# In two layer norms, the copy that forms the second 16-bit part of each row moves from ScalarE to GpSimd

## What is computed

```python
edge_index = jnp.stack([src, dst])
xn = _layernorm(x, axis=-1)
x = x + _L0_gnn_ref(xn, edge_index, ...) + _L0_mix_ref(xn[None], ...)[0]
x = x + _L0_ffn_ref(_layernorm(x, axis=-1)[None], ...)[0]
xn = _layernorm(x, axis=-1)
x = x + _L1_gnn_ref(xn, edge_index, ...) + _L1_mix_ref(xn[None], ...)[0]
x = x + _L1_ffn_ref(_layernorm(x, axis=-1)[None], ...)[0]
return x
```

## Time and profile before

| | us |
|---|---|
| median of 3 runs | 4698.83 (4697.29 to 4701.39) |
| the profiled execution | 4690.14 |
| its span in the trace | 4688.2 |
| PE busy | 3698.4 (79% of the span) |
| DVE busy | 2192.3 (47%) |
| ACT busy | 1351.2 (29%) |
| POOL busy | 744.5 (16%) |

### The profile page before, as it was taken

How to read it: one execution, slowest core, us unless ns; L and a number is a source line. 1 busy time by engine, 2 the same in 40 slices (tenths; PEclk the granted TensorE clock), 3 DMA queues, 4 the chain that set the end, 5 groups by cost and what they waited for, 6 DMA issues and landing times. The chain is left out here.

```text
span 4688.2 us, 90793 instructions
## 1 busy us (share of the span) xinstructions
PE 3698.4 (79%) x23358; PEld 2637.5 (56%) x23359; DVE 2192.3 (47%) x5705; ACT 1351.2 (29%) x2984; POOL 744.5 (16%) x1224
## 2 busy tenths in 40 slices
PE   4888864899699989972464539749989899789998
PEld 2444433566388579651344326529879544457776
DVE  7888878888700221251253420260040577723333
ACT  2555632777600100320010212330000125233333
POOL 3222200000000000017323460200000365200000
PEclk9999975778799899975787769869999999989999
DMA  2111220322244035111010121214425200010000
GB/s 104 49 74 74 93 83 0 97 86 86 86 154 150 32 125 190 35 26 43 11 53 4 41 26 42 92 69 173 165 93 186 73 1 1 5 29 7 13 13 27
DMA packets 128991, 318.06 MB, mean 68 GB/s; under 512 B 46782, under 2 KB 80045, under 8 KB 114376
## 3 DMA queue, kind: packets, MB, share of 16 engines
q1 hardware_dynamic: 113664, 300.41, 18.4%
q0 software_dynamic: 11808, 9.68, 1.6%
q10 hardware_dynamic: 3404, 6.53, 0.4%
HBM read 244.26 MB, written 72.46 MB: 68 GB/s over the span
## 5 line engine op out<-in xcount | busy, mean ns | idle before, releaser
L555 PE MATMUL ps<-hot_key,hot_src 128*126 128x512 bf16 (+1 forms) x2208 | 416.4, 314 | 38.9 <-DVE hot_key L520 20.9
L520 DVE TENSOR_SCALAR hot_key<-col_iota,run_keys 128x625 bf16<-128x625 int16 x1104 | 393.9, 379 | 0.0
L2437 PE MATMUL ps<-xnT,ew 128*128 (+2 forms) x640 | 208.8, 482 | 203.9 <-issue 120.8
L1336 PE MATMUL ps<-gnn_u_thirds,near 125*128 125x256 bf16 x3000 | 336.0, 275 | 23.1 <-issue 23.1
L1336 PEld LDWEIGHTS ps<-gnn_u_thirds,near 125*128 125x128 bf16 x3000 | 330.4, 141 | 27.0 <-issue 24.7
L555 PEld LDWEIGHTS ps<-hot_key,hot_src 128*126 128x126 bf16 x2208 | 212.4, 136 | 234.3 <-DVE hot_key L520 171.6
L2437 PEld LDWEIGHTS ps<-xnT,ew 128*128 128x128 f32 x640 | 132.6, 213 | 274.9 <-issue 151.7
L2312 POOL DMA_INDIRECT rows_room<-node_table,src_idx x256 | 260.9, 1019 | 141.3 <-issue 141.3
L517 DVE TENSOR_SCALAR hot_src<-col_iota,run_srcs 128x125 bf16<-128x125 int16 x828 | 211.6, 256 | 97.0 <-PE ps L555 56.1
L864 PE MATMUL ps<-row_hot,slot_hot 128*128 128x512 f16 x1088 | 221.4, 356 | 3.1 <-DVE row_hot L1077 2.6
L2471 PE MATMUL ps<-table_thirds,rows_room 125*128 125x144 bf16 x1728 | 127.7, 231 | 108.9 <-issue 67.7
(11 more groups left out here) (564 smaller groups left out, 6655.2 us busy)
## 6 DMA issues: line engine op xcount, KB each, us to landing
near<-adjacency SPq DMA_DIRECT2D x80, 1562.5 KB, 6.6
adjacency<-counts SPq DMA_DIRECT2D x125, 312.5 KB, 2.2
own_in<-own_rows SPq DMA_DIRECT2D x34, 512.0 KB, 4.0
expert_rows<-rows_y SPq DMA_DIRECT2D x75, 125.0 KB
rows_room<-expert_rows SPq DMA_DIRECT2D x25, 375.0 KB
pair_in<-high_rows SPq DMA_DIRECT2D x34, 256.0 KB
pair_in<-low_rows SPq DMA_DIRECT2D x34, 256.0 KB
agg0a_adj<-adjacency SPq DMA_DIRECT2D x5, 1562.5 KB, 9.7
```

Of the source, the lines that this page charges most:

```text
L520: nc.vector.tensor_scalar(hot_key[:, j, :], col_iota[:], run_keys[:, ds(at, 1), j:j + 1].rearrange("p a j -> p (a j)"), None, ALU.is_equal ...
L555: last = nc.tensor.matmul(sums[:, b:e], hot_src[:, j, :], hot_key[:, j, b:e], start=False, stop=True, skip_group_check=True)
L1336: last = nc.tensor.matmul(ps[:, j, 0:width], lead_tiles[BUF[j]][:, k, :], parts.thirds[:, k, i, :], start=(k == 0 and i == 0), stop=(k == ...
L2437: last = nc.tensor.matmul(ps[:, piece % 2, 0:n], w1[i][:, c, m * 128:(m + 1) * 128], xnT[:, c, ds(g * NG + first, n)], start=(c == 0), sto ...
```

## The change

ACT no longer makes the second part. POOL gets an instruction list in these two stages: for each tile it waits until the remainder is made, copies it rounded to bf16, and signals DVE. The operands, the semaphores and DVE's instructions are the same.

```diff
                         if t >= 1:
                             b = t - 1
-                            act.wait_ge(left_out, b + 1)
-                            nc.scalar.activation(third(1, b), parts.left[:, b % TG, :],
-                                                 ACT.Copy).then_inc(second_out, 1)
                             act.wait_ge(transposed, b + (TG + 1))
                             nc.scalar.activation(xnT[:, :, b * P:(b + 1) * P],
...
-                if pool_program:
+                if parts:
+                    @block.gpsimd
+                    def _(pool):
+                        for t in range(T):
+                            pool.wait_ge(left_out, t + 1)
+                            nc.gpsimd.tensor_copy(third(1, t), parts.left[:, t % TG, :]).then_inc(second_out, 1)
+                elif pool_program:
                     block.gpsimd(pool_program)
```

## The result

The changed kernel takes 4683.12 us, median of 6 runs (4678.27 to 4686.86), against 4698.32 for the kernel before in the same comparison (4694.38 to 4702.94, 6 runs): a ratio of 0.9968, with a 95% interval of 0.9958 to 0.9978, or 15.2 us less. It was forecast at 4684.0, with a range of 4680.5 to 4692.

A forecast was written before the change was run, and what follows sets the result against it. ACT was taken to bound both norms; without its copy ACT and DVE each need 1.06 us per tile, saving 7.6 us per norm, 15.2 in all. From median 4698.83 to 4683.6, with jitter 4684.0 us; range 4680.5 to 4692.

The forecast's parts named there:

- S: Copy of the remainder into the second 16-bit part (L1245), 0.31 us of ACT's period per tile, moved to POOL.
- The cover of the copy: From remainder's end to DVE's last part 0.98 us, of which POOL's wake-up, copy and return need 0.58: 0.40 us spare.
- B: DVE's remainder (L1200), both inputs in SBUF; 0.48 us, expected to stay so beside POOL's copy.
- C: DVE's last part (L1206), both inputs in SBUF, waiting for the copy; expected to start 0.23 us ahead of POOL.
- The hold: Delay per tile when DVE and POOL read SBUF side by side: taken as 0, bounds 0 and the whole copy, 0.40.
- A: DVE's normalised row (L1193), the step ahead of the remainder; 0.32 us from its start to the remainder's.
- partial hold: Rival: POOL's copy starts or ends late, each remainder waits 0.05 to 0.20 us; 4685 to 4691.6 us; 15%.
- 1249.95 + 21p: End of a norm's last turned-tile copy if DVE alone decides, p its period per tile; 1272.2 at p = 1.06.
- X: ACT's copy of the turned tile (L1248); the last one sets the norm's end, forecast 7.6 us earlier per norm.
- The first rival: SBUF port pair held for whole durations, 1.31 to 1.37 us per tile: 4693.4 to 4695.8 us; 11%.
- The slower one: Rival: POOL gets operands first in every tile and its copy stands in DVE's chain: 4699.6 to 4706.4 us; 5%.
- POOL late: Rival: POOL's new instructions arrive only behind the adjacency tiles, first last-part step waits 4 us: 4691.6 us; 4%.

The follow-up runs named there:

- experiment 1: Changed kernel without POOL's copies, second part zero, DVE's last step reading the first part instead: 1.059 us per tile by DVE's normed row, 1.056 by ACT's first part.
- experiment 3: Kernel before, normed row in two 128-column halves: 0.341 us against 0.407 whole. Changed kernel, plain numbers for per-row ones: 0.484 us beside POOL, period 1.133.
- experiment 2: Changed kernel with POOL still copying, but DVE's last step reads the first part and doesn't wait for the copy: 1.133 us per tile, normed row 0.483.
- experiment 5: Changed kernel with POOL copying only columns 0 to 127 of each remainder, the rest zero: normed row 0.408 us, period 1.056 to 1.059 us.

## Why the prediction was right, and where it wasn't

**What bounds the norm**: right. Taking S from ACT shortened the tile, and the spill's 4.1 us at the end stayed.

**ACT's 1.06 and DVE's 1.06 without POOL**: right, by experiment 1 (1.056 and 1.059).

**The cover of the copy, 0.40 us**: right. POOL woke 0.06 us after B (0.15 was taken), took 0.53 for the copy (0.5 was expected beside DVE), and C never waited for it but once per norm, at the very end. The copy ended 1.06 us after B's start, near the 1.10 of the forecast.

**The hold, taken as 0**: wrong by 0.073 us per tile (1.133 against 1.06). It is the term that was mis-sized. The prediction looked for instructions that POOL can hold and took those with two SBUF inputs, B and C; it laid out their reading against S and found that it just fitted ahead of B. That part held good: B stayed at 0.47 but for one at either end of the norm (0.54 and, with no A ahead of it, 0.61). A, which has one input, was left out, and it stands right where S reads. It reads at double speed (experiment 3), and experiments 1, 2, 3 and 5 show that it is the one that is held. The Trainium skill names such a case (SBUF — State Buffer, section "SBUF: two separate sides"): the lock is also met by a DVE operation in a two-port performance mode. The profile doesn't name modes, but the trace agrees: A at double speed takes 0.48 beside S and 0.41 without it. It doesn't agree on a hold of whole durations, since of A's 0.48 all but 0.15 ran beside S. Two signs lay in the trace of before. The copy L3021, with one input, took 0.23 or 0.69. And A took 0.41 where B took 0.48; but two per-row numbers cost A 0.12 us by experiment 3, and by its length it looked like single speed. The sign that was named for a partial hold, B at 0.55 or more, could not have shown this one.

The line 1249.95 + 21p was sound. With p = 1.133 it puts the last X at 1273.7; shifted by the 0.7 us by which this norm started earlier, 1273.0, and it ended at 1273.10. So 7.6 us per norm should have been 6.4, and 15.2 in all 12.8. By mechanism this is the second rival, the partial hold, with the hold on another instruction than was thought, and its time would have been 4686, 4698.8 less 12.8.

**The measured 15.2 us** equals the forecast's sum by luck. 12.8 of it lie in the norms, in both traces of the changed kernel, from two chips. The other 2.4 are within the scatter of the runs: 12.8 lies within both intervals (10 to 20 us, and 9 to 22 us on the second chip), and the spans of the two profiled executions differ by 11.6 us. No run shows a cause for them. The time alone can't tell the forecast from the partial hold; the rows can.

**The first rival** (whole durations exclude each other, 1.31 to 1.37 us): out, by 1.133 and by experiment 5 (1.059 with a copy of 0.43 us). **The slower one**: out; C starts 0.14 us ahead of S in the steady tile, less than the 0.23 of the forecast, since POOL woke sooner. **POOL late**: out; its first copy began 0.07 us after the first B. **The copy isn't what held DVE**: out; without ACT's copy the idle time ahead of C is gone.

## What to carry to other kernels

When a copy moves from ACT to POOL beside a busy DVE, list every DVE instruction that POOL can hold. In these runs they were those with two SBUF inputs (B, and L3008 in the earlier trace rows) and those with one input that run from SBUF to SBUF at double speed (A, L3021); a sum with one input at single speed (L3005) was not held. Find the speed from two sizes of one instruction, not from its length. Then lay out the reading parts alone, not the durations: POOL's copy was free while its columns fitted between two of them, and what it went beyond that was paid by the instruction behind, tile for tile.

## What the runs showed of the hardware

- A held DVE instruction ended its own reading time and 0.02 us more behind POOL's end: 0.15 us for 256 columns at double speed (A), 0.27 at single speed (B), 0.08 for 128 columns at double speed (L3021). Its fixed part ran while it was held, whether that is 0.27 us (two per-row numbers) or 0.15 (plain numbers).
- POOL is held likewise: a copy of 0.40 us alone took 0.53 behind C and ended 0.26 behind C's end; one of 128 columns took 0.43 and ended 0.15 behind it.
- The kernel took 4695 to 4698 us on some chips and 4334 to 4340 on others. The norms were equal to 0.02 us on both kinds (27.88 to 27.89 us for the changed kernel). The difference lies between the first norm and the second: 1877 us from one to the other on the slower chips, 1510 in experiment 3 on a faster one. Its cause stays open.
